# A graph network with its nodes renumbered by block, and a rebuilt stage change between gated layer and recurrence

## The reference

```python
src = randint(0, 6250, (100000,))
dst = minimum((6250 * uniform((100000,)) ** 2.0).astype(int32), 49999)   # then both sorted by dst

# layer 0, three times:      agg = segment_sum(h[src], dst); h = h + agg; two dense layers with batch norm and relu
# layer 1, gated:            att = sigmoid(x[src] @ W_att[:d] + x[dst] @ W_att[d:] + b_att)
#                            agg = segment_sum((x[src] @ W_msg + b_msg) * att, dst); one GRU step
#                            gamma * (h - mean over nodes) * rsqrt(var over nodes + eps) + beta
# layer 2, recurrence:       h = enc(x); five times: m = h @ w[i]; agg = segment_sum(m[src], dst); GRU(agg, h)
#                            sigmoid(dec(relu(h)))
# layer 3:                   segment_sum(x[src], dst) @ W.T + b
```

## Time and profile before

| | |
|---|---|
| three timed runs | median 4018.3 us (4017.14 to 4019.05) |
| profiled execution | 4019.86 us; its span 4017.6 us |
| granted TensorE clock, mean | 0.994 |
| PE busy | 3710.6 us, 92% of the span |
| DVE busy | 2909.2 us, 72% |
| ACT busy | 2512.6 us, 63% |
| POOL busy | 304.7 us, 8% |
| HBM traffic | 397 MB read, 44 MB written |

### The profile page before, as it was taken

The page is one execution under the profiler, slowest core; times in us unless marked ns, Lnnn a source line. Parts: engine busy times, 40 slices in busy tenths (PEclk is TensorE's granted clock), DMA queues, the critical chain, the costliest instruction groups (busy, mean ns, idle before and its releaser), DMA issues.

```text
span 4017.6 us, 57803 instructions
## 1 busy us (share of the span) xinstructions
PE 3710.6 (92%) x16970; PEld 2906.7 (72%) x16970; DVE 2909.2 (72%) x6934; ACT 2512.6 (63%) x4580; POOL 304.7 (8%) x658
## 2 busy tenths in 40 slices
PE   0148889999999999999899999999999999999999
PEld 0126678888888545555688888888888888888887
DVE  9999956656667788887676766666666676677755
ACT  1039856666666787777566556655655655666665
POOL 0011100000023110000330000000000000033300
PEclk9999999999999999999899999999999999999999
DMA  3039954555544332221254444444444444434444
GB/s 65 0 138 366 366 162 136 159 139 141 159 132 121 100 82 72 72 63 47 77 140 118 126 138 127 117 137 135 120 133 136 120 119 137 125 102 116 118 135 136
DMA packets 361521, 515.39 MB, mean 128 GB/s; under 512 B 159908, under 2 KB 228253, under 8 KB 360824
## 3 DMA queue, kind: packets, MB, share of 16 engines
q1 hardware_dynamic: 340572, 458.67, 40.4%
q0 software_dynamic: 7696, 46.93, 3.2%
q10 hardware_dynamic: 12938, 6.05, 0.7%
HBM read 396.98 MB, written 43.87 MB: 110 GB/s over the span
## 4 chain that ended last, share of the span: by engine, by line
PE 49%; POOL 1%; ACT 1%; DVE 1%; issue 0%; DMA 0%; SPq 0%; ACTq 0%; POOLq 0%; DVEq 0%
PE ps L2270 40%; PE ps L2382 3%; PE ps L2383 3%; PE ps L2385 1%; PE ps L2384 1%; ACT wide L2108 0%; PE ps L2367 0%; PE ps L2308 0%; PE ps L2302 0%; PE ps L2411 0%; PE ps L2406 0%; POOL inv L2179 0%; PE ps L2293 0%; PE ps L2285 0%; POOL root L2178 0%
## 5 line engine op out<-in xcount | busy, mean ns | idle before, releaser
L2270 PE MATMUL ps<-wide,hi 128*128 128x512 f32 (+2 forms) x5537 | 2149.7, 391 | 12.3 <-DVE lo L2604 7.7
L2270 PE MATMUL ps<-wide,lo 128*128 128x512 f32 (+2 forms) x5537 | 2075.7, 379 | 0.0
L2108 DVE CAST wide<-ring 128x1024 fp32r<-128x1024 uint8 (+1 forms) x1274 | 1001.7, 786 | 617.3 <-PE ps L2270 610.9
L2108 ACT CAST wide<-ring 128x1024 fp32r<-128x1024 uint8 (+1 forms) x1274 | 1237.0, 971 | 3.0 <-DMA ring<-count 2.3
L2270 PEld LDWEIGHTS ps<-wide,hi 128*128 128x128 f32 x5537 | 1041.9, 188 | 212.9 <-issue 18.5
L2270 PEld LDWEIGHTS ps<-wide,lo 128*128 128x128 f32 x5537 | 1043.0, 188 | 190.3
L2465 ACT CAST hi<-high 128x128 fp32r<-128x128 f32 x1274 | 380.8, 299 | 922.3 <-PE ps L2270 517.0
L2266 PE MATMUL ps<-hN,hB 128*128 128x512 f32 (+1 forms) x1274 | 522.9, 568 | 3.0 <-DVE aggT L2428 1.7
L2458 ACT ACTIVATE hN<-aggT,source_scores 128x512 f32<-128x512 f32 (+1 forms) x637 | 427.7, 694 | 115.0 <-PE ps L2266 83.6
L2586 DVE TENSOR_TENSOR hN<-hN,ring 128x512 f32<-128x512 f32 (+1 forms) x637 | 400.8, 666 | 101.6 <-ACT hN L2458 96.1
L2266 PEld LDWEIGHTS ps<-hN,hB 128*128 128x128 f32 x1274 | 241.0, 190 | 262.1 <-issue 208.2
(11 more groups left out here) (246 smaller groups left out, 3333.8 us busy)
## 6 DMA issues: line engine op xcount, KB each, us to landing
ring<-count SPq DMA_DIRECT2D x490, 320.0 KB, 3.0
ring<-count SPq DMA_DIRECT2D x441, 256.0 KB, 2.7
ring<-count SPq DMA_DIRECT2D x490, 224.0 KB, 2.6
wide<-aggT POOLq DMA_DIRECT2D x49, 896.0 KB, 6.5
count<-aggT SPq DMA_DIRECT2D x49, 800.0 KB, 4.0
hB<-mid SPq DMA_DIRECT2D x192, 32.0 KB, 1.9
hN<-mid SPq DMA_DIRECT2D x192, 32.0 KB, 1.9
hB<-squares SPq DMA_DIRECT2D x96, 32.0 KB, 2.0
```

The lines of the kernel that those rows point to most:

```text
L2108: return copy(wide[:, g % WIDE_SLOTS, c0:c1].rearrange("p (t u f) -> p t u f", u=2, f=P), rows[:, g % row_slots, c0:c1].rearrange("p (t f ...
L2270: ins = e.matmul(ps[:, c, 0:size], part[:, g % CUT_SLOTS, :], wide[:, g % WIDE_SLOTS, w0:w0 + size], start=k == 0 and part is hi, stop=k = ...
```

## The change

1. **Node numbers.** Node v now stands at place v + 22: block (v + 22) div 128, row (v + 22) mod 128. The 22 pads are the first rows of block 0. Keys are made by shifts and masks on integers; `near`, `part`, `low`, `moved` and the ACT operation between the loads are gone. The bucket is made of the blocks as before, and has the same room. The states are loaded and the result is stored in rows of 512 bytes.
2. **Pads out of the sums.** The first chunk of the first third loses 22 of its 384 columns (`unused`), in the products and in the copies behind them.
3. **End of the counts.** The last source block's columns of the early sum are widened by ACT and DVE instead of a DMA, `many` is computed behind the last sums, and the first two rows of counts (`ROWS_AHEAD`) are fetched before the first pipeline begins.
4. **Stage change.** The `w_steps` products, and the batch norm's factors (on DVE, with one power on POOL), move in front of the barrier. In the head of the recurrence the inverse root is made by DVE but for the power, and the chunks are encoded two steps earlier (`ENTER`).

```diff
@@ sort_edges @@
-            e.tensor_scalar(near[:, :, :], edges[:, :, :], float(NB // 2), 1.0 / NB, ALU.subtract, ALU.mult)\
-            e.tensor_scalar(part[:, :, :], near[:, :, :], MAGIC, MAGIC, ALU.add, ALU.subtract)\
-            e.scalar_tensor_tensor(low[:, :], part[:, 0, :], -float(NB), edges[:, 0, :], ALU.mult, ALU.add).then_inc(ch.sem, ch.up())
-            e.scalar_tensor_tensor(field[:, :], part[:, 1, :], float(P), part[:, 0, :], ALU.mult, ALU.add).then_inc(ch.sem, ch.up())
...
+            e.tensor_scalar(places[:, 1, :], edges[:, 1, :], float(PADS + KEY_BIAS * P), None, ALU.add).then_inc(ch.sem, ch.up())
+            e.tensor_scalar(places[:, 0, :], edges[:, 0, :], float(PADS), None, ALU.add).then_inc(ch.sem, ch.up())
+            e.tensor_scalar(target_row[:, :], places[:, 1, :], 7, (P - 1) << 7, ALU.logical_shift_left, ALU.bitwise_and).then_inc(ch.sem, ch.up())
+            e.tensor_scalar(blocks[:, :, :], places[:, :, :], 7, None, ALU.logical_shift_right).then_inc(ch.sem, ch.up())
+            e.scalar_tensor_tensor(field[:, :], places[:, 0, :], P - 1, target_row[:, :], ALU.bitwise_and, ALU.bitwise_or).then_inc(ch.sem, ch.up())
+            e.scalar_tensor_tensor(bucket[:, :], blocks[:, 0, :], float(2 * NCHUNK), blocks[:, 1, :], ALU.mult, ALU.add).then_inc(ch.sem, ch.up())
@@ fill_counts @@
+        def widen_last(copy, b0, b1):
+            return copy(wide[:, (NB - 1) % EARLY_SLOTS, b0:b1], rows[(NB - 1) % ROW_BUFFERS].bitcast(U8)[:, c0 + b0:c0 + b1]).then_inc(s["widened"], 1)
...
-            e.wait_ge(s["added"], 1)
-            e.tensor_scalar(many, ps[:, TURN, P:P + 1], float(BG * P * P - E) + 0.5, None, ALU.is_gt)
...
+            for k in range(ROWS_AHEAD):
+                e.dma_start(first_rows[:, k, :], count[k * P:(k + 1) * P, 0:ROW_BYTES]).then_inc(s["ahead"], 16)
@@ Flow.run @@
-ENTER = {"normal": 0, "turned": 0, "added": 2, "root": 3, "even": 5, "back": 5, "plain": 7, "coded": 7, "code": 9, "encoded": 10, "entered": 12, "source": 12}
+ENTER = {"normal": 0, "turned": 0, "added": 2, "root": 3, "even": 3, "back": 3, "plain": 5, "coded": 5, "code": 7, "encoded": 8, "entered": 10, "source": 10}
...
+            def unused(q, c):
+                return PADS if q == 0 and c == 0 else 0
...
-                                ins = e.matmul(ps[:, c, 0:size], part[:, g % CUT_SLOTS, :], wide[:, g % WIDE_SLOTS, w0:w0 + size],
+                                ins = e.matmul(ps[:, c, u0:size], part[:, g % CUT_SLOTS, :], wide[:, g % WIDE_SLOTS, w0 + u0:w0 + size],
...
-                        inverse_root(y, t, m, mv[u][:, 0:c.blocks, 1])
-                        e.tensor_tensor(y, y, t, ALU.mult).then_inc(s["rooted"], 1)
+                        e.tensor_tensor(inv[u][:, 0:c.blocks], root[u][:, 0:c.blocks], net.root_power[:, 0:c.blocks], ALU.pow).then_inc(s["powered"], 1)
```

More of the change, by code:

```diff
@@ L238, in sort_edges @@
         ends = net.hN[:, 0:3 * 2 * EDGE_L].rearrange("p (t n l) -> p t n l", t=3, l=EDGE_L)[0:EDGE_P]
-        edges, near, part = ends[:, 0].bitcast(I32), ends[:, 1], ends[:, 2]
-        low = sb("low", [EDGE_P, EDGE_L])
-        moved = sb("moved", [EDGE_P, EDGE_L])
+        edges, places, blocks = (ends[:, i].bitcast(I32) for i in range(3))
+        target_row = sb("target_row", [EDGE_P, EDGE_L], I32)
         field = sb("field", [EDGE_P, EDGE_L], I32)
         bucket = sb("bucket", [EDGE_P, EDGE_L], I32)
-        key_bias = sb("key_bias", [P, 1])
         A, B = ([net.aggT[:, (2 * n + b) * FREE:(2 * n + b + 1) * FREE] for b in (0, 1)] for n in (0, 1))
@@ L573, in fill_counts @@
     assert len(pieces) == groups == 4
-    names = ["left", "apart", "right", "mm", "out", "spread", "normal", "turned", "state", "high", "hi", "lo", "summed", "whole", "copied", "absent", "added",
+    names = ["left", "apart", "right", "mm", "out", "spread", "normal", "turned", "state", "high", "hi", "lo", "summed", "whole", "copied", "widened", "ahead", "absent", "added",
              *[f"loaded{j}" for j in range(EARLY_SLOTS)]]
@@ L729, in _ @@
                 cut(j)
+            e.wait_ge(s["out"], groups * (NB - 1) + last_group)
+            e.wait_ge(s["summed"], NB - EARLY_SLOTS)
+            widen_last(e.copy, EARLY_COPIED, middle)
         @block.gpsimd
         def _(e):
-            for k in range(NB):
+            for k in range(NB - 1):
                 if k >= EARLY_SLOTS:
@@ L1798, in _ @@
                 stores = 0
-                whole = out[0:FULL_P * NB, :].rearrange("(p k) f -> p (k f)", k=NB)
-                rest = out[FULL_P * NB:N, :].rearrange("(a k) f -> a (k f)", a=1)
                 for i in range(NSLAB):
@@ L1869 @@
     bn: object
+    gamma: object
+    beta: object
+    weights: object
+    steps: int
+    w_in: list
 @dataclass(frozen=True)
@@ L2056, in run, with counts_of, loaded, bank_of @@
             rows = ring[:, 0:row_slots * ROW_BYTES].rearrange("p (j f) -> p j f", f=ROW_BYTES)
-            if self.enter is not None:
-                c0, size = row_slots * ROW_BYTES, self.enter.steps * 3 * D * 4
+            ahead = ROWS_AHEAD if self.given else 0
+            first_rows = net.rows_ahead()
+            def counts_of(g):
+                return first_rows[:, g, :] if g < ahead else rows[:, g % row_slots, :]
+            def loaded(e, g):
+                if g >= ahead:
+                    e.wait_ge(s[f"row{g % row_slots}"], (g // row_slots + 1 - (g % row_slots < ahead)) * 16)
+            prepared = layers[-1] if attends else None
+            if self.enter is not None or attends:
+                steps = self.enter.steps if self.enter is not None else prepared.steps
+                c0, size = STEP_ROW_SLOTS * ROW_BYTES, steps * 3 * D * 4
                 combined = ring[:, c0:c0 + size].bitcast(F32).rearrange("p (n g f) -> p n g f", g=3, f=D)
-                turned_w = net.aggT[:, 0:self.enter.steps * D]
+                turned_w = net.aggT[:, 0:steps * D]
             def combined_at(g):
-                n, odd = divmod(g - self.head[2].at, 2) if self.enter is not None else (0, 1)
-                return [n] if not odd and 0 <= n < self.enter.steps else []
+                n, odd = divmod(g - total - PREPARE["product"], PREPARE["apart"])
+                return [n] if attends and not odd and 0 <= n < steps else []
+            def bank_of(n):
+                return (4, 7, 2, 3)[n % 4]
             def gates_of(c):
@@ L2370, in _ @@
                             gru = self.step(c)
-                            if self.enter is not None and c.turn == 1:
-                                e.wait_ge(s["w_kept"], self.enter.steps)
                             if attends and c.turn == 1:
@@ L2898, in program @@
                           att_rep[:, :], scores, source_scores, messages)
-            Flow(net, [layer_scales(n) for n in range(layers0 - 1)] + [leave, Attend(gated, scores, source_scores, states_bn[:, :])],
+            Flow(net, [layer_scales(n) for n in range(layers0 - 1)] + [leave, Attend(gated, scores, source_scores, states_bn[:, :], gam[:, :], bet[:, :], w_steps, steps, wt("2ih"))],
                  add_self=True, given=(EARLY,)).run()
```

266 lines of the change are left out of this document (148 added, 118 removed).

## The result

The changed kernel takes 19,831 us (median of four runs, 19,828 to 19,836) against 4018.3 us before: 4.93 times as long, 95% interval 4.928 to 4.941. The forecast was 21,000 in a range of 17,500 to 26,000. The second path runs, behind a first path that is some 9 us shorter than before and whose output is overwritten.

The account below looks back on a forecast made before the run. PE's columns of products bound the pipelines, but overfull 128-place buckets decide: the first path's 4,009 us plus the second path's 16,950 give 20,960, said as 21,000 us, range 17,500 to 26,000.

Parts of the forecast that it names:

- The 128 places: Buckets of 128 places: block 0 puts 266 edges in each; 12,865 edges lack a place, so the second path runs.
- All or nothing: The limit of `many`: one edge without a place decides whether the second path runs.
- The sum of the second path: Zeroing, adds, half rows, 27 sums, `attend` and the rest: 16.95 ms, bounds 13.5 and 22.7.
- The half rows: Second path: 98 half rows cut into bytes, each behind its barrier, 28 us each, 2.8 ms; bounds 2.1 and 3.9.
- 784 × 1.3: Second path's indirect adds on POOL: 1.02 us each and 0.3 between two, within a stage of 1.3 ms.
- The bound of 2,400: Upper bound in us for the second path's 784 indirect adds, with nothing beside anything.
- The first path: Parts 1 to 4 without the second path: sum −9.4 us, giving 4009 us.
- The stage change's terms: Moved `w_steps` products, batch norm factors and recurrence head: together +10.9 us, bounds −2 and +25.
- the key chain: DVE's seven key operations, three of them with 800 columns instead of 1600: −1.6 us; smaller memset −0.7.
- The end of the counts: Before the first pipeline, without the transfer in both places: first product about 508.5 instead of 516.71 us, −8.1.
- near 1,965 us: Sign to look for in the first path: when the `high` of the recurrence would come.
- Rival 3: Second path off, DVE the bound in all 38 steps and the fetch ahead winning nothing: 4,032 us, slower; chance 0.005.

Follow-up runs that it names:

- e1: The changed kernel with the limit of `many` raised out of reach, so the second path never runs; 4010.9 us against 4020.2 for the kernel before.
- e2: The kernel before, own numbering, with the limit of `many` lowered so the second path always runs; 19,834.8 us.
- e4: The changed kernel with nodes dealt out over the blocks from row 22 on, fullest bucket 118, limit untouched; 4017.0 us against 4020.2.
- e3: The changed kernel with its pads kept but nodes dealt out in turn, leaving 27 edges without a place; 19,837.4 us.
- e8: The changed kernel in full, but the second path's 784 indirect transfers write their amounts instead of adding them; 19,160.5 us.
- e5: e1's kernel with the recurrence head's inverse root back on POOL and the encoding two steps later; 4001.5 us, ratio 0.9954.
- e9: The changed kernel, but in the second path DVE's compares wait until POOL's adds of the group before have landed; 20,672 us.

## Why the prediction was right, point by point

- **The 128 places.** Right, and it decided everything: e1, e2 and e4 turn the second path off and on by the limit alone or by the numbering. The argument needed no row: the share of edges below a node, the number of source blocks, and the room of a bucket.
- **All or nothing.** Right: e3's 27 edges cost the full price.
- **The sum of the second path.** 16,950 forecast, 15,832 measured. The sums were overrated: 60 us for clearing, filling and draining each, where the window of one aggregation shows PE busy 867 of 903 us, so 12 a sum; 301 us instead of 345. The 285 below the 60 were right (289); the 60 had no row behind them. `attend` was read from a stretch that also held GRU products, 640 a plane instead of 538; my low bound came from the same stretch and was too high: a tuned stretch's length is the sum of all that is packed into it, not that of the piece that gives it its name. That the whole lies within 7% of the forecast is partly luck: the adds took 632 us more than forecast, the other five pieces 1,750 less.
- **The half rows.** 27.6 us each, 28 forecast, though with errors that cancel. One half row and the begin of the next, DVE and the issues of SP:

```profile
7012.56 0.35 SPq L955 DMA_DIRECT2D g_wide<-exact  x1
7018.65 1.76 DVE L971 CAST whole_i<-g_wide 128x3072 int32<-128x3072 f32 x1 [11.78 <-DMA g_wide<-exact]
7020.45 1.76 DVE L973 TENSOR_SCALAR digit<-whole_i 128x3072 int32<-128x3072 int32 x1
...
7031.41 0.33 SPq L961 DMA_DIRECT2D count<-cut  x1
...
7036.99 0.35 SPq L955 DMA_DIRECT2D g_wide<-exact  x1
7043.17 1.89 DVE L971 CAST whole_i<-g_wide 128x3328 int32<-128x3328 f32 x1 [6.12 <-DMA g_wide<-exact]
7045.10 1.89 DVE L973 TENSOR_SCALAR digit<-whole_i 128x3328 int32<-128x3328 int32 x1
7047.02 3.62 DVE L975 CAST cut<-digit 128x3328 uint8<-128x3328 int32 x1
```

The narrow half passes at 0.57 ns a column throughout; in the wide one the three casts to bytes take 3.62 us for 3,328 columns, 1.09 ns each, nearly twice as long, which I had not seen coming. Against it the wait for the load is some 6 us, start included, under the 7.4 I had, and from the first store to the next load's issue pass 5.6 us, where store and barrier had 6.9.
- **The adds.** The failed step is "784 × 1.3": an indirect read's 1.02 us was taken for an add's. An add keeps POOL for 1.82 us in the mean, 2.12 with the 0.30 between two, so that term is 1,660 us instead of 1,020. The other term held: what the stage leaves for the wait at the end of a group is 2.8 us, 3 in the forecast. The prediction feared a price outside POOL's row, in the landing; it lies in the row. (The landing of 2.9 us beside which it set the 1.02 was another transfer's; the ten reads' own, in the trace of before, is 2.8 to 3.3.) The bound of 2,400 held it. The Trainium skill, "DMA: Bandwidth & Descriptors", Specifications, has transfers under 512 bytes done by reading, changing and writing. But e8's writes are of 4 bytes as well and cost POOL 0.96 us; the size alone is not what the adds pay for here.
- **The first path.** 4009 forecast, 4010.9 against 4020.2 measured, −9.3 by the runs against −9.4. That they agree to 0.1 is luck: by the spans it is −11.2, and 2 us behind the span that no term foresaw bring it back. The stage change's terms also add up to +10.7, not to the +10.9 written. Its terms: the key chain, three rows of seven,

```profile
6.69 0.58 DVE L303 TENSOR_SCALAR hN<-hN 125x800 int32<-125x800 int32 x1 [2.16 <-DMA hN<-in_dst]
...
8.28 0.99 DVE L307 TENSOR_SCALAR hN<-hN 125x1600 int32<-125x1600 int32 x1
...
11.23 0.99 DVE L312 SCALAR_TENSOR_TENSOR aggT<-bucket,field 125x800 int32<-125x800 int32 x1
```

6.69 to 12.22 us instead of 6.76 to 13.66, −1.4 where −1.6 was forecast. Three operations at half of 0.99 are −1.5, not −1.6. The start is only 0.07 earlier, not 0.7: it waits for the edges. The end of the counts,

```profile
501.43 2.48 DVE L653 TENSOR_TENSOR aggT<-ps,hT 128x512 f32<-128x512 f32 x4 [1.96 <-PE ps L691]
...
503.83 0.15 DVE L657 TENSOR_SCALAR many<-ps 128x1 int32<-128x1 f32 x1
...
505.36 1.04 ACT L2146 CAST wide<-aggT 128x1024 fp32r<-128x1024 uint8 x1
...
506.55 0.57 PE L2290 MATMUL ps<-wide,hi 128*128 128x362 f32 x1 [3.77 <-ACT wide L2146]
```

the first product at 506.55 instead of 516.71 in this run, 507.4 in e1: −9.3 to −10.2 for both terms, forecast −10.4. From there to the end of the first pipeline, the aggregate at 1928.23 below, pass 1,421.7 us where it had been 1,425.6: −3.9, where pads, `attend` and the moved products of `w_steps` were to give −2.7 − 1.8 + 1.9. The barrier,

```profile
1928.23 1.48 DVE L2694 BATCH_NORM_AGGREGATE states_bn<-hN 128x2 f32<-128x294 f32 x1
...
1931.61 0.16 DVE L2704 TENSOR_TENSOR states_bn<-bet,states_bn 128x1 f32<-128x1 f32 x1
1934.34 0.29 DVE L2742 TENSOR_TENSOR xN<-ps,xN 128x128 f32<-128x128 f32 x1 [2.56 <-PE ps L2303]
...
1956.63 0.22 DVE L2653 TENSOR_SCALAR high<-hN 128x128 int32<-128x128 int32 x1
```

28.4 us from the aggregate to the first `high` where it had been 24.7: +3.7, forecast −0.7 + 4.1. (The sign "near 1,965 us" for this `high` contradicts the terms, which put it at 1957.4; it starts at 1956.63.) In the steps 5.97 against 5.65, forecast 6.03 against 5.68. The number is right and its make-up is not: five operations at 0.27 us were to add 1.35; by the rows of e1 and e5 DVE works 5.31 us a chunk against 4.65, so they add 0.66, and the other 0.66 is DVE's wait for POOL's power, which this term left out. Rival 3's "not in 19 but in all 38 steps" names one thing twice, since a chunk lasts two steps. The head's loss was seen, 4.1 + 5.4 = 9.5 us in the forecast and 9.4 by e5; that this made the moved root a loss, and its undoing the better kernel, follows from the same terms, and the prediction didn't draw the conclusion.

## What to carry to other kernels

Before the instructions of a renumbering are counted, ask which structure has a fixed size, how full it was, and what the kernel does when it runs over: two lines of arithmetic on the data's distribution outweighed every row of the trace. A numbering by remainder is not there for its own sake; it spreads a skewed input, and a fallback that has never run has no row that would warn. Where work goes from an idle engine to the one that sets a stretch's pace, count the whole cycle of that stretch, with the waits of the hand-over: five operations of 0.16 us and a wait of 0.66 us for POOL used up a slack of 1.0 us.

## What the runs showed of the hardware

- An indirect transfer of 128 rows keeps POOL for 0.96 us as a write of 4 bytes a row into HBM (e8), 1.02 as a read of windows of 384 keys, and 1.55 as an add of 4 bytes a row. An add that follows another while DVE compares takes 2.11 us in the middle (370 of 784 in the changed kernel, all above 1.7; none in e9, where the longest of all took 1.75).
- A cast to bytes took 0.57 ns a column at 3,072 columns and 1.09 at 3,328 (147 of each). The first writes 12 pairs of blocks, the second 13; why the wider is slower was not tried.
- Zeroing moved 413 GB/s over 386 us, against 365 in the busiest window of the earlier trace rows.
